# One GpSimd multiplication of 2048 columns in place of two of 1024, in three of eight units of a selective scan

## What is computed

```
x = x + 0.5 * ffn(layernorm(x))      # 8 experts of 344, top 2 of 8 by a router
x = x + mamba(layernorm(x))          # 4 layers, then Wout and bout
x = x + 0.5 * ffn(layernorm(x))      # the same weights again

# one layer of mamba, 256 inner channels, 16 states a channel
dA  = exp(delta * A);  dBu = (delta * u) * B
h_t = dA_t * h_(t-1) + dBu_t         # the scan, over the 512 tokens
y_t = sum over the 16 states of h_t * C_t
y   = (y + u * Dp) * silu(z);  x = x + y @ Wblk
```

## Time and profile before

| | |
|---|---|
| median of 3 runs | 4565.08 us (4559.62 to 4566.4) |
| profiled execution: span from first to last instruction | 4554.2 us |
| profiled execution: its own time | not among the times shown |
| POOL busy | 4093.5 us (90%) |
| DVE busy | 4047.9 us (89%) |
| PE busy | 3939.2 us (86%) |
| ACT busy | 3342.2 us (73%) |
| mean granted TensorE clock | 0.951 |

### The profile page before, as it was taken

How to read it: one execution, slowest core, us unless ns; L and a number is a source line. 1 busy time by engine, 2 the same in 40 slices (tenths; PEclk the granted TensorE clock), 3 DMA queues, 4 the chain that set the end, 5 groups by cost and what they waited for, 6 DMA issues and landing times.

```text
span 4554.2 us, 48397 instructions
## 1 busy us (share of the span) xinstructions
PE 3939.2 (86%) x11712; PEld 1280.3 (28%) x11712; DVE 4047.9 (89%) x5505; ACT 3342.2 (73%) x5047; POOL 4093.5 (90%) x1804
## 2 busy tenths in 40 slices
PE   7886777998999999899998999999899989678769
PEld 2221222232322323232232323223232323122223
DVE  2668898999999999999999999999999999889963
ACT  4566776777777777777778777777777777667734
POOL 0559999999999999999999999999999999999960
PEclk9897887999999999999999999999999999789969
DMA  2233544354434444544454445444444554444410
GB/s 72 61 78 95 115 106 98 85 118 110 97 87 112 107 93 99 114 104 96 98 112 96 97 101 119 95 97 101 112 92 89 117 113 91 101 99 95 99 41 5
DMA packets 154562, 434.46 MB, mean 95 GB/s; under 512 B 16429, under 2 KB 53230, under 8 KB 153903
## 3 DMA queue, kind: packets, MB, share of 16 engines
q1 hardware_dynamic: 154287, 431.36, 41.4%
HBM read 150.28 MB, written 12.58 MB: 36 GB/s over the span
## 4 chain that ended last, share of the span: by engine, by line
POOL 41%; issue 16%; DVE 14%; PE 12%; ACT 8%; DMA 3%; SPq 2%; DVEq 0%; ACTq 0%; POOLq 0%
POOL work L909 21%; POOL work L900 19%; DVE work L720 5%; DVE dA_ps L720 4%; SPq L363 2%; PE d_ps L434 2%; PE s_ps L481 2%; DVE work L725 2%; DMA bc_sb<-bc_rows 2%; ACT sg_sb L583 2%; ACT L583 1%; PE b_ps L427 1%; ACT dA_ps L556 1%; DMA dd_sb<-dd_src 1%; ACT L584 1%
## 5 line engine op out<-in xcount | busy, mean ns | idle before, releaser
L909 POOL TENSOR_TENSOR work<-dd_sb,bc_sb 128x2048 f32<-128x2048 f32 x512 | 2319.6, 4531 | 72.4 <-DMA dd_sb<-dd_src 72.2
L556 ACT ACTIVATE dA_ps<-dd_sb,a_sb 128x512 f32<-128x512 f32 x2048 | 1369.2, 684 | 643.1 <-DVE work L725 542.9
L900 POOL TENSOR_TENSOR work<-work,bc_sb 128x1024 f32<-128x1024 f32 x704 | 1655.9, 2359 | 35.1 <-DVE work L720 34.7
L720 DVE TENSOR_TENSOR_SCAN work<-dA_ps,work 128x512 f32<-128x512 f32 x1408 | 1646.7, 1203 | 40.7 <-POOL work L909 32.0
L720 DVE TENSOR_TENSOR_SCAN dA_ps<-dA_ps,work 128x512 f32<-128x512 f32 x640 | 780.9, 1220 | 10.9 <-ACT dA_ps L556 5.1
L434 PE MATMUL d_ps<-sg_sb,wd_sb 128*128 128x512 f32 (+1 forms) x1536 | 721.0, 601 | 18.8 <-DVE sg_sb L805 18.8
L405 PE MATMUL y_ps<-work,sel_sum 128*32 128x512 f32 x4096 | 580.3, 640 | 81.9 <-POOL work L900 53.7
L421 PE MATMUL a_ps<-xT_sb,wg_sb 128*128 128x512 f32 (+1 forms) x768 | 439.5, 655 | 87.1 <-ACT sg_sb L583 80.7
L421 PE MATMUL b_ps<-xT_sb,wg_sb 128*128 128x512 f32 (+1 forms) x768 | 434.5, 648 | 92.2 <-ACT sg_sb L583 87.8
L725 DVE TENSOR_TENSOR work<-dA_ps,bc_sb 128x512 f32<-128x512 f32 x640 | 435.8, 681 | 8.3
L427 PE MATMUL a_ps<-xs_sb,wu_sb 128*128 128x512 f32 (+1 forms) x768 | 412.2, 619 | 20.7 <-DVE sg_sb L805 16.2
(11 more groups left out here) (116 smaller groups left out, 3823.6 us busy)
## 6 DMA issues: line engine op xcount, KB each, us to landing
dd_sb<-dd_src SPq DMA_DIRECT2D x512, 512.0 KB, 8.5
bc_sb<-bc_rows SPq DMA_DIRECT2D x256, 512.0 KB, 5.8
xr_sb<-in_L_attn_x SPq DMA_DIRECT2D x16, 256.0 KB, 3.3
bc_rows<-dbc_sb SPq DMA_DIRECT2D x128, 32.0 KB, 1.7
x<-xr_sb SPq DMA_DIRECT2D x16, 256.0 KB, 3.6
xr_sb<-x SPq DMA_DIRECT2D x16, 256.0 KB, 2.9
out<-xr_sb SPq DMA_DIRECT2D x16, 256.0 KB, 2.3
wg_sb<-in_L_ffn_Wg SPq DMA_DIRECT2D x1, 1376.0 KB
```

The source lines that it names most:

```text
L556: act.activation(dA_ps[:, g % NDA, :], dd_sb[:, b, c, 0, :], ACT.Exp, scale=a_sb[:, l, b, j, c:c + 1]).then_inc(dA_ready, 1)
L720: dve.tensor_tensor_scan(dA if on_dve(i) else tile, dA, tile, 0.0, ALU.mult, ALU.add).then_inc(scanned, 1)
L900: pool.tensor_tensor(work[:, g % RING], work[:, g % RING], bc_sb[:, j, 0, :].unsqueeze(1).broadcast_to([128, 2, T]), ALU.mult).then_inc(po ...
L909: pool.tensor_tensor(work[:, g % RING:g % RING + 2].rearrange("p h c t -> p (h c) t"), dd_sb[:, b, :, 1, :], bc_sb[:, j, 1, :].unsqueeze(1 ...
```

## The change

In the units in which DVE multiplies nothing (1, 4 and 7), POOL issues one product over both halves, at offset 29 + 16u, where the second half stood. It waits for all four scans of the unit and adds 2 to the semaphore of the products. The other units keep their instruction of 1024 columns. Nothing else differs.

```
-CORE = {"exp": -10, "scan": -1, "dbu": -3, "dve_prod": 0, "pool_prod": 21, "sum": 30, "y0": 87, "y1": 8}
+CORE = {"exp": -10, "scan": -1, "dbu": -3, "dve_prod": 0, "pool_prod": 21, "pool_unit": 29, "sum": 30, "y0": 87, "y1": 8}
...
             def core_pool(t):
-                if (at := part_at(t, CORE["pool_prod"], 8)) and not (at[2] % 2 == 1 and at[2] // 2 in DVE_UNITS):
+                if (at := part_at(t, CORE["pool_prod"], 8)) and at[2] // 2 in DVE_UNITS and at[2] % 2 == 0:
                     k, w, i = at
                     j, g = (i // 2) % NJ, HALVES * k + i
                     pool.wait_ge(scanned, 2 * g + 2)
                     pool.tensor_tensor(work[:, g % RING], work[:, g % RING],
                                        bc_sb[:, j, 0, :].unsqueeze(1).broadcast_to([128, 2, T]), ALU.mult).then_inc(pool_prod, 1)
+                if (at := part_at(t, CORE["pool_unit"], 16)) and at[2] not in DVE_UNITS:
+                    k, w, u = at
+                    j, g = u % NJ, HALVES * k + 2 * u
+                    pool.wait_ge(scanned, 2 * g + 4)
+                    both = work[:, g % RING:g % RING + 2].rearrange("p h c t -> p (h c) t")
+                    pool.tensor_tensor(both, both, bc_sb[:, j, 0, :].unsqueeze(1).broadcast_to([128, NG, T]),
+                                       ALU.mult).then_inc(pool_prod, 2)
                 if at := part_at(t, CORE["dbu"], 16):
```

## The result

The changed kernel took **4601.2 us** (median of 4 runs, 4595.14 to 4605.59) against 4562.35 for the kernel before on the same chips (4 runs, 4557.17 to 4566.4): ratio 1.0086, 95% interval 1.0072 to 1.0101. It is slower by some 39 us. The forecast was 4584 in a range of 4549 to 4618, slower with a chance of 0.62: the time is in the range and the sign is right, but the rise is twice the one forecast (18.7 us). The profiled spans are 4593.4 after and 4554.2 before, so 39.2 us apart, and can be compared row by row.

A forecast was written before the change was run, and what follows sets the result against it. The prediction saw coupled rings of POOL, VectorE and TensorE, decided by slack at each crossing, with POOL's 35 us saving off the path. Holds 18.8 less ScalarE 4.1 plus ends 4 gave +18.7, so 4584 us, range 4549 to 4618.

The forecast's parts named there:

- One instruction of 2048 columns lasts as a `dbu`: Merged C product on POOL: 4.48 us from distances of starts, against 4.66 for two old ones, saving 35 us of POOL.
- POOL is 2.15 us late in unit 4: Unit 4 of router phases: the product waits for the fourth scan and ends at 2025.97, where the second half ended at 2023.82.
- The router hides this: Before the router, POOL comes 2.15 us later but without the first half's 2.32, so the router starts 0.17 earlier.
- Unit 7 is late, and y is held: Whole product behind the router ends 2.18 us late each router phase; TensorE's sum starts 1.48 late and VectorE's y is held.
- A hold of 1.10 and 0.47 us: VectorE's y in the two kinds of router phase, 12 of each in the regular stretch: 18.8 us together.
- ScalarE gives 4.1 us back: ScalarE's small exponential waits for the router's first instruction and regains up to 0.17 us in 24 router phases: 4.1 off.
- The two ends cost 4 us: Outside the regular stretch, eight router phases and gains elsewhere: bounds -4 and +17, taken as +4, nearer to a mixture.
- gains of 0.18: Each merge saves POOL 0.18 us; at the ends a phase gains 3 x 0.18 = 0.5 where POOL is behind.
- Rival 1: POOL is the bound and the wait only moves its phase: faster, 4530, or 4548 if only some phases profit; chance 0.18.
- rival 2: Nothing moves: POOL's gain is waited away and VectorE makes up for the held y; 4565 give or take 9; chance 0.2.
- rival 3: Shift paid in full: y and D hold VectorE by 2.18 us in all 32 router phases, 70 us, 4635; chance 0.1.
- The base: Median of the runs, 4565.1 us, 10.9 above the profiled span of 4554.2, put down to what lies around it.

The follow-up runs named there:

- merge 1: Kernel before with only unit 1 merged and moved to the new place, units 4 and 7 as before: 4586.6 us, ratio 1.0054.

## Why the prediction was right, and where it was short

- *One instruction of 2048 columns lasts as a `dbu`.* Right: 4523 ns for 4531. The Trainium skill (GPSIMD Engine Reference, section "Elementwise — side-by-side cycle accounting") leaves some 60 ns fixed by the prediction's estimate from its two figures; the rows of the changed kernel give 2 x 2360 - 4523 = 197 ns, so the trace differs.
- *POOL is 2.15 us late in unit 4, and stops for scans grow to over 100 us.* Right but for a hair: 99.7 us, 110 times.
- *The router hides this, since it no longer has the first half of unit 7 ahead.* Right, shown from both sides: either the new order or the new wait alone costs more than the whole (54 and 126 us for 39).
- *Unit 7 is late, and y is held.* Right in kind and place: stops before y in the regular stretch 5 to 29 times; 47.6 us over the whole span for "some 40". A microsecond more at that place is shown to count, and at unit 2 to be free.
- *A hold of 1.10 and 0.47 us.* Too small, and this is the first term of the sum that was mis-sized: 1.53 and about 0.9, measured at seams without a spell of half clock. The prediction let y's slack of 0.38 soften the lateness of the sum. But TensorE is an in-order engine too: its own lateness, 2.18 - 0.70 = 1.48 in one kind of phase and 2.18 - 1.33 = 0.85 in the other, reaches VectorE whole through the gate product (24 stops before `xs_sb` for 2). These two numbers are within 0.05 of what was measured.
- *ScalarE gives 4.1 us back.* ScalarE's stops for the router's first instruction did shrink, from 28.7 to 25.4 us, but nothing of it is in the delay of VectorE: VectorE's stop before the experts' product fell from 0.66 to 0.21 in the phase shown, and the one before y took this up. Together the regular stretch was forecast at 18.8 - 4.1 = 14.7 us and lost 25.7.
- *The two ends cost 4 us.* They cost 7.9 + 5.6 = 13.5, inside the bounds of -4 and 17, near the upper. A mixture of gains and losses was the wrong choice: at the start three late units 7 cost 2.16 us or more each, and from 535 to 623 us of the changed kernel, where no router stands, the delay stays at 2.30 us, so the gains of 0.18 are waited away. At the end the delay grows in part at y and in part at scans that wait for `dbu`. With the two points above this makes up the missing 20 us: 25.7 - 14.7 = 11.0 and 13.5 - 4 = 9.5.
- *Rival 1, POOL bounds*, is refuted by the time and by the microsecond at unit 2, *rival 2* by the time, *rival 3* by the time and by VectorE's stops for `dbu`, which didn't grow in the regular stretch (10.4 us for 10.7) and little over the whole span (36.1 for 32.0).
- *The base.* The prediction put the 10.9 us between the profiled span and the median down to "what lies around it". The runs list span and time of one execution: 4593.4 and 4595.14, 1.7 us apart. So the profiled execution of the kernel before took some 4556 us, a little less than the fastest of the four listed. This moved no term, since the median was the base anyway.

The time fell in the range although the rise was forecast at half its size, because the range was wide enough on that side. No large errors cancelled: two terms were too low, and one was wrongly taken off.

What stays open: how much of merge 1 and of the kernel merged where no router follows is the clock alone, what the saved work of POOL is worth, and that no kernel that shortens or moves the late wait won the time back.

## What to carry to other kernels

An instruction that replaces two gives its result when the second would, and waits for what the second waited for: look up who waits for the first half, and what was issued in between. When such a late product enters another in-order engine, count the lateness of that engine's whole queue; a consumer's own slack is only good for that one way. An engine at 98% busy can still be the one that waits: one dummy instruction, put at the suspected place and then at a slack one, tells in two runs. A place that costs nothing in one phase can hand its lateness to the next: follow it until a stop takes it up.

## What the runs showed of the hardware

- A stop of TensorE of 2.52 us and one of 3.11 us were each followed by a granted clock of about half; one of 1.90 us in the changed kernel was followed by a convolution at full speed (3.70 us). At half clock the products took 1.91 us for 1.02 and the convolution 5.40 for 3.70. The length of the last stop alone doesn't tell: in the kernel before, the clock was at half from 1388.4 us on, behind a stop of 1.00 us, and the chain of two products took 1.98 us for 1.13 at the same place in the kernel with unit 1 merged, behind a stop just as long:

```profile
1388.23 1.98 PE L473 MATMUL s_ps<-xpad,mean_w 128*128 128x512 f32 x2 [1.00 <-DVE lg_sb L832]
```

```profile
1395.85 1.13 PE L474 MATMUL s_ps<-xpad,mean_w 128*128 128x512 f32 x2 [1.00 <-DVE lg_sb L833]
```

- A microsecond more on one path can cost more than a microsecond: 26.7 us more of stops before y came with 17.7 us more before the gate product, behind products at half clock, and the time rose by 45 us.
- The small power instruction on POOL (4 columns) took 1037 ns, five times as long as the multiplication of 4 columns beside it (202 ns).
- The merged product works in place and took 4523 ns, 11 ns less than the `dbu` product of as many columns that reads another tile: writing over its own input made no difference worth counting.
